# Leaving out the dummy identity products in the head and the tail of a three-block transformer kernel

## What is computed

```python
def ffn(x, W_fc, W_proj):
    h = jnp.square(jax.nn.relu(jnp.einsum('bsd,fd->bsf', x, W_fc)))
    y = jnp.einsum('bsf,df->bsd', h, W_proj)
    # five steps of a leaky membrane driven by y; the spikes are counted
    _, spks = jax.lax.scan(step, zeros_like(y), None, length=5)
    return jnp.sum(spks, axis=0) / 5

x = x + 0.5 * ffn(layernorm(x), W_fc, W_proj)
x = x + attention(layernorm(x), w_qkv, w_out, b_out)   # causal, softmax, 16 heads
x = x + 0.5 * ffn(layernorm(x), W_fc, W_proj)
```

## Time and profile before

| | |
|---|---|
| median of 3 runs | 1568.95 us |
| lowest and highest | 1568.69 and 1569.36 us |
| profiled execution: its time | 1571.02 us |
| profiled execution: its span, first to last instruction | 1569.2 us |
| busy: PE, DVE, ACT, POOL | 1547.5, 1102.2, 1301.9, 928.3 us |
| PE matmul instructions | 10399 |
| mean granted clock of TensorE | 0.998 |

### The profile page before, as it was taken

The page is one execution under the profiler, slowest core; times in us unless marked ns, Lnnn a source line. Parts: engine busy times, 40 slices in busy tenths (PEclk is TensorE's granted clock), DMA queues, the critical chain, the costliest instruction groups (busy, mean ns, idle before and its releaser), DMA issues.

```text
span 1569.2 us, 33807 instructions
## 1 busy us (share of the span) xinstructions
PE 1547.5 (99%) x10399; PEld 1252.8 (80%) x10399; DVE 1102.2 (70%) x4091; ACT 1301.9 (83%) x3497; POOL 928.3 (59%) x1255
## 2 busy tenths in 40 slices
PE   8999999999999999999999999999999999999998
PEld 7778878887887888888788788878888878888776
DVE  6576776676776677776677766767776777766745
ACT  6888888888887888888888888888888888888884
POOL 4556656666665566556656566666655665566552
PEclk9999999999999999999999999999999999999999
DMA  4454454444455445444444544444554454444540
GB/s 119 91 115 105 98 121 99 105 107 101 107 111 113 98 92 118 108 105 105 104 109 98 121 99 103 107 102 105 111 115 98 94 120 104 102 105 102 114 103 20
DMA packets 80194, 163.10 MB, mean 104 GB/s; under 512 B 12816, under 2 KB 30864, under 8 KB 79888
## 3 DMA queue, kind: packets, MB, share of 16 engines
q1 hardware_dynamic: 80016, 160.94, 47.2%
HBM read 6.88 MB, written 4.19 MB: 7 GB/s over the span
## 4 chain that ended last, share of the span: by engine, by line
PE 96%; DVE 2%; ACT 1%; issue 1%; POOL 0%; POOLq 0%; DVEq 0%
PE bank L497 19%; PE bank L483 18%; PE bank L469 12%; PE bank L470 10%; PE bank L449 8%; PE bank L450 7%; PE bank L453 7%; PE bank L544 7%; PE bank L554 2%; PE bank L555 2%; PE bank L557 2%; PE bank L527 1%; ACT prob L1149 1%; PE bank L646 1%; PE bank L564 0%
## 5 line engine op out<-in xcount | busy, mean ns | idle before, releaser
L1350 POOL TENSOR_TENSOR prob<-prob,rsum 128x512 f32<-128x512 f32 (+3 forms) x1024 | 746.3, 742 | 583.7 <-DVE rsum L805 581.4
L1149 ACT ACTIVATE prob<-negsc,negmax 128x512 f32<-128x512 f32 (+3 forms) x1024 | 576.8, 566 | 164.6 <-DVE negmax L796 162.6
L796 DVE CUSTOM_DVE_ANT_0 negsc<-bank,dist 128x512 f32<-128x512 f32 (+3 forms) x1024 | 467.5, 475 | 0.3 <-issue 0.3
L805 DVE RECIPROCAL rsum<-sums 128x1 f32<-128x1 f32 (+1 forms) x768 | 123.4, 161 | 399.5 <-PE bank L470 382.4
L1162 ACT COPY probT<-bank 128x512 f32<-128x512 f32 x635 | 355.5, 587 | 46.4 <-PE bank L483 40.6
L483 PE MATMUL bank<-ident,prob 128*128 128x128 f32 x2540 | 356.1, 273 | 0.5 <-POOL prob L1350 0.3
L469 PE MATMUL bank<-keys,queries 128*128 128x256 f32 (+2 forms) x1024 | 350.3, 353 | 2.1 <-issue 2.0
L483 PEld LDWEIGHTS bank<-ident,prob 128*128 128x128 f32 x2540 | 299.1, 140 | 28.7 <-POOL prob L1350 5.6
L470 PE MATMUL bank<-keys,queries 128*128 128x256 f32 (+2 forms) x1024 | 319.7, 324 | 0.0
L497 PE MATMUL bank<-probT,vals 128*64 128x512 f32 x2032 | 301.5, 439 | 0.2 <-DVE queries L920 0.2
L497 PEld LDWEIGHTS bank<-probT,vals 128*64 128x64 f32 x2032 | 134.4, 136 | 159.6 <-issue 124.6
(11 more groups left out here) (143 smaller groups left out, 2190.1 us busy)
## 6 DMA issues: line engine op xcount, KB each, us to landing
queries<-queries SPq DMA_DIRECT2D x381, 256.0 KB, 2.9
keys<-k_lo SPq DMA_DIRECT2D x254, 128.0 KB, 2.4
keys<-keys SPq DMA_DIRECT2D x127, 128.0 KB, 2.3
x_in<-in_L_attn_x_dram SPq DMA_DIRECT2D x16, 256.0 KB, 3.1
out_dram<-x SPq DMA_DIRECT2D x15, 256.0 KB, 2.7
prob<-in_L_attn_w_qkv_dram SPq DMA_DIRECT2D x1, 1024.0 KB, 7.4
prob<-in_L_attn_w_qkv_dram SPq DMA_DIRECT2D x1, 512.0 KB, 8.2
probT<-in_L_attn_w_out_dram SPq DMA_DIRECT2D x1, 512.0 KB, 9.4
```

Source lines behind the costliest of these rows:

```text
L796: ins = dve.tensor_tensor_reduce(negsc[:, k % 3, col:col + WIDTH[i]], src, dist[:, N - WIDTH[i]:N], SLOPES[2 * p + h], MASKED, ALU.add, AL ...
L805: dve.reciprocal(rsum[:, p % 2, cols], sums[:, p % 2, cols]).then_inc(s_rsum, 1)
L1149: ins = act.activation(prob[:, p % 2, h, PCOL[i]:PCOL[i] + WIDTH[i]], negsc[:, k % 3, col:col + WIDTH[i]], ACT.Exp, bias=negmax[:, p % 2, ...
L1350: ins = pool.tensor_tensor(pr, pr, rsum[:, p % 2, seg:seg + 1].to_broadcast([P, WIDTH[i]]), ALU.mult)
```

## The change

All eight calls of `keep_warm` and the helper are left out: 41 products in the head and 14 in the tail, 110 matmul instructions with their weight loads. No wait, no other instruction and no order is changed.

```diff
-            def keep_warm(count, warm_bank=out_bank):
-
-                for _ in range(count):
-                    pe.matmul(warm_bank[:, 0:P], ident[:, :], ident[:, :], start=True, stop=True)
-
...
                 pe.wait_ge(s_const, 2)
-                keep_warm(9)
...
                 weights_turn(s_wfc, fc_raw, score_bank[0])
-                keep_warm(6, first_bank[0])
                 block_by_halves(1, 0, ((s_wfc_lo, 1), (s_wproj_out, 1)), lambda: weights_turn(s_wproj, proj_raw, score_bank[1]))
-                keep_warm(8, end_turn_bank[1])
                 pe.wait_ge(s_block_half, 1)
-                keep_warm(10, score_bank[0])
                 for half in range(2):
...
                     mm.then_inc(s_first_half["xT2"] if half == 0 else s_xT[2], 1)
-                    keep_warm(3 - half, score_bank[0])
                 pe.wait_ge(s_xhi[2], 1)
...
                 pe.wait_ge(s_wsecond, 2)
-                keep_warm(3)
...
                     last_out_turn(half)
-                keep_warm(14, score_bank[1])
                 block_by_halves(3, b, None)
```

## The result

The changed kernel takes 1574.2 us (median of 6 runs, 1572.19 to 1574.68) against 1568.82 us before (median of 6, 1568.01 to 1569.36). The ratio is 1.0032, with a 95% interval from 1.0021 to 1.0042: 5.4 us slower. Measured once more, it was 1573.41 against 1569.29 us, ratio 1.0028 (1.0018 to 1.0038): 4.1 us slower.

What follows compares the result with a forecast made beforehand. TensorE was taken to bound the kernel, carrying 96% of the chain. Losses of 1.8 (start), 2.0 (head pause), 0 (first slot) and 2.2 (tail) sum to 6.0 us on 1568.95: 1575.0 us, range 1570.4 to 1579.0.

Steps and rivals of the forecast that it cites:

- The start: First block of the head: without 9 and 6 dummies TensorE runs it slow for 4.0 to 5.7 us; 1.8 us lost.
- The 0.4 us gain: Ahead of the first block: TensorE could take xn at 7.14 us instead of 7.56, at most 0.4 us gained.
- The pause in the head: Between first block and first slot: a 4.9 us wait drops the clock, slowing the 512-column products; 2.0 us lost.
- The first slot: TensorE's existing 3.73 us wait for the next batch's xn moves later; costed at 0, between -2.6 and +0.8 us.
- Rival 4: First slot: late, slow head products fill TensorE's wait, the clock holds, 2.6 us come off; 1572.4 us, chance 0.07.
- The tail: Last batch's block: 3.45 us idle without 14 dummies drops the clock, slowing the block; 2.2 us lost, ends 0 and 6.3.
- the nearness of 3.45 to 2.66 us: Tail: the 3.45 us idle lies nearer 2.66 us, after which the clock fell, than 5.2, so a fall was assumed.
- The dummies do not hold the clock: Head and tail: neither pause drops the clock, only the start loses 1.4 to 2.2 us; 1570.8 us, chance 0.08.
- One of the two pauses does not bring the clock down: Head pause or tail keeps full clock; 1572.8 us without the tail's loss, 1573.0 without the head pause's; chance 0.16.
- faster: Head: full clock in real work, block 0.4 us earlier, shorter first-slot pause worth 2.6 us; 1566.0 us, chance 0.02.
- Slow for longer: Both blocks: short waits inside keep the clock down, up to 14.6 us; halfway 10 us, 1579 us, chance 0.07.
- the loop changed its length by more than a microsecond: Loop between first slots and tail: expected as long as before; a change above a microsecond would prove the forecast wrong.

Runs made afterwards that it cites:

- the thin dummies: All 55 dummies of the kernel before kept, each with 8 moving columns instead of 128; 1574.68 us, ratio 1.0038.
- the first execution: The changed kernel, all dummies left out against the kernel before, in its first profiled execution; 1573.03 us.
- the mean of five: Five profiled executions of the changed kernel, without further edit; 1573.03, 1572.84, 1573.62, 1576.83 and 1573.71 us, mean 1574.0.
- the three kernels: Each puts one group of dummies back into the changed kernel: before the first block 1572.16, head pause 1571.65, tail 1571.01 us, against 1568.68 before.
- after_look2: The changed kernel once more with no edit, one time and one profile; 1576.83 us.
- after_look1: The changed kernel once more with no edit, one time and one profile; 1573.62 us.

## Why the prediction was right, and where its steps were off

The direction and the range held: 1574.2 us against 1575.0 forecast (1570.4 to 1579.0). The mechanism, that what the dummies give is the clock, is shown by the thin dummies and by the stages in which one group was put back. The size came out closer than its terms were: three of the four were too high against the traces, whose sum is 3.7 us, and the first measurement, 5.4 us, happens to lie above that sum. The second, 4.1 us, is farther from the 6.0. So the closeness was in part luck.

- *The start*, forecast 1.8 us, measured 0.9 in the first execution (15.86 to 16.76), 1.1 on the mean of five, and 0.9 by the three kernels. This term was mis-sized. The 0.4 us gain is there. PE was slow for about 3.6 us of the block (7.17 to 10.8) in that execution, and for 4.0 to 4.5 in the other four, by the pace of the products: near the low end of the 4.0 to 5.7 us assumed, or under it. And not all of that counts at 0.46 us a microsecond. From the transposes to the first product it is 8.87 - 7.17 = 1.70 us against 8.49 - 7.56 = 0.93 in the kernel before: 0.77 us lost, what 0.46 us a microsecond gives. From there to the second matrix it is 2.37 us, 1.9 of them slow, against 1.79: 0.58 lost, not 0.9. In the kernel before PE does not set the pace there: its products start 0.20, 0.17 and 0.23 us apart (8.49 to 9.09) before they come 0.12 apart, and slow products hide such waits. Together 1.35, less 0.39, is 0.96 us.
- *The pause in the head*, forecast 2.0 us, measured 1.9 to 2.3 from the end of the block to the first slot (13.97 to 14.33 us against 12.05); 1.4 by the three kernels, with the uncertainty named there. Right, in the size and in the way: the 5.03 us wait brings the clock down, and the products of 512 columns carry it to VectorE's low halves.
- *The first slot*, costed at 0 with bounds of -2.6 and +0.8, measured from -0.2 to -2.3 us, -1.3 on the mean. The step that put this at nothing is the one that failed. Rival 4 had the size (-2.6) and not the reason: PE's wait was not filled by late work, it is 3.74 us long in each of these executions. What changed is whether and when the clock falls in it; why it does in one execution and not in another stays open.
- *The tail*, forecast 2.2 us, measured 1.2 to 2.3, 1.6 on the mean; 2.1 by the three kernels. The clock fell in all five executions, as forecast, but the nearness of 3.45 to 2.66 us was no sound reason for it: a longer wait, the 3.74 us of the first slot, left the clock up in two of the same executions. The spread of this term comes from where the slow stretch lies against the block: in the first execution it began 2.5 us before PE went on and ended 4.3 us after, in after_look2 it began only 0.4 us before and ended 6.4 us after.
- *The sum.* The terms on the mean of five traces give 1.1 + 2.1 - 1.3 + 1.6 = 3.5 us, and 0.2 in the loop, where the medians give 4.1 and 5.4. So 6.0 was above what the traces have, and the 5.4 us near to it are not all explained by the stages; the term that was too high by most is the first slot's. The execution of 1576.83 us is the case that the forecast described, with a head of 31.79 - 27.95 = 3.8 us, almost nothing given back and 2.3 us in the tail. It is one of the longest.
- *The rivals.* "The dummies do not hold the clock" fell with the pause and the tail. "One of the two pauses does not bring the clock down" fell with the five traces, which have a slow stretch in both. Of "faster", the 0.4 us at the start showed, and the first slot without a slow stretch in two executions, but never full clock from the start of the first block. "Slow for longer" did not come: the longest execution of the changed kernel took 1577.52 us, under its 1579.

The forecast said that it would be wrong if the loop changed its length by more than a microsecond. It varies that much between executions of the same kernel (1299.89 and 1298.78 us before), so that sign was too fine; on the mean it stayed (1299.5 against 1299.3).

The Trainium skill, "TensorE: Matmul & The Clock Gate", Part 1, says that the number of slow products at the start differs from run to run of one kernel. The traces agree: PE is slow for 3.6 to 4.5 us of the first block of the changed kernel, and the first dummies take 3.80 to 4.21 us. The first slot varies more, with 0, 3.4 or 6.8 us of slow clock behind one and the same wait.

## What to carry to other kernels

Where the first and last stages of a kernel wait for other engines, look at the pace of like instructions and at the granted clock on both sides of each wait, and cost a slow stretch only for the part in which TensorE sets the pace. Dummies were worth here what the clock was worth in the work right behind them, about 0.9 to 2.1 us a place; full-size products gave that, those of 8 columns did not, and those that ended after the real work was due held it up. A stretch of slow clock that moves can also shrink elsewhere, so follow the delay through the next stages before adding up.

## What the runs showed of the hardware that was not expected

- The clock fell between 0.7 us (after_look1: PE's last transposes before the pause of the tail end at 1553.37 us, the fall is at about 1554.07) and 5.2 us after PE's last work. A single distance read from one trace is no bound. The stretch of that fall:

```profile
1553.80:1554.20 0.40, 0.00 (x0) 0.00 (x0) 0.36 (x3) 0.00 (x0) 0.00 (x0) 0.84 0.00 0
```

- It can fall after PE has begun again: in the first execution after, PE goes on at 40.24 us and the clock is down from about 41.5 us, with PE busy all through.
- The same 3.74 us wait was followed by a fall of the clock in three executions of the changed kernel and by none in two.
- Products of 8 columns, with as many weight loads and as much time on the engine as full ones, neither brought the clock up (the next twelve in 2.57 us) nor held it (0.50 from 23.2 us).
- The granted clock of the profile reads 1.00 from the start to the first recorded change, also where like instructions run at half the pace (0.21 us between products of 256 columns at 9.7 us, while the column has 1.00).
